# Two-layer decoder, second pass: the scores for the cross-attention maxima issued per lane instead of per pair

## What is computed

```python
logits = jnp.einsum('bhqd,bhkd->bhqk', q * SCALE, k)
logits = jnp.where(mask[:, None, None, :], -jnp.inf, logits)
attn = jax.nn.softmax(logits, axis=-1)
out = jnp.einsum('bhqk,bhkd->bhqd', attn, v)
```

## Time and profile before

| | us |
|---|---|
| median of 3 runs (3334.25 to 3343.13) | 3335.63 |
| the profiled execution | 3339.14 |
| its span, first to last instruction | 3337.6 |
| PE busy | 3049.2 (91%) |
| DVE busy | 2039.0 (61%) |
| ACT busy | 1907.7 (57%) |
| second pass, about | 915 to 2258 |

### The profile page before, as it was taken

How to read it: one execution, slowest core, us unless ns; L and a number is a source line. 1 busy time by engine, 2 the same in 40 slices (tenths; PEclk the granted TensorE clock), 3 DMA queues, 4 the chain that set the end, 5 groups by cost and what they waited for, 6 DMA issues and landing times. The chain is left out here.

```text
span 3337.6 us, 82480 instructions
## 1 busy us (share of the span) xinstructions
PE 3049.2 (91%) x31903; PEld 2442.6 (73%) x31903; DVE 2039.0 (61%) x6892; ACT 1907.7 (57%) x6449; POOL 387.0 (12%) x457
## 2 busy tenths in 40 slices
PE   6999999999888989898989898975999989999998
PEld 5777777777675757575757575754888878888886
DVE  3666667666546364646464646454677766767775
ACT  2665556665544545454545444444677767777775
POOL 1112211122000000000000000000111111111111
PEclk8999999999999999999999999986999999999999
DMA  3000000000020101010101010005001122020100
GB/s 118 17 15 17 12 13 15 17 14 20 19 66 9 33 9 33 9 33 9 33 9 33 9 33 10 9 7 202 16 15 19 17 60 61 16 63 15 18 16 10
DMA packets 63711, 95.77 MB, mean 29 GB/s; under 512 B 6962, under 2 KB 58754, under 8 KB 61778
## 3 DMA queue, kind: packets, MB, share of 16 engines
q1 hardware_dynamic: 54946, 82.74, 7.8%
q0 software_dynamic: 8368, 7.70, 1.9%
HBM read 72.04 MB, written 18.37 MB: 27 GB/s over the span
## 5 line engine op out<-in xcount | busy, mean ns | idle before, releaser
L1581 PE MATMUL bps<-BXT,Bwexp 128*128 128x112 f32 x3072 | 377.4, 279 | 6.5 <-DMA Bwexp<-in_we 4.2
L1581 PEld LDWEIGHTS bps<-BXT,Bwexp 128*128 128x128 f32 x3072 | 364.9, 195 | 16.9 <-issue 7.1
L1699 ACT ACTIVATE BPT<-bps,Blow 112x112 f32<-112x112 f32 x1024 | 350.6, 440 | 39.2 <-DVE Blow L1814 39.2
L1345 DVE CUSTOM_DVE_ANT_0 PON<-pps,PMR 112x375 f32<-112x375 f32 x512 | 251.5, 545 | 127.8 <-PE pps L1080 127.8
L1699 ACT ACTIVATION_READ_ACCUMULATOR BPT<-bps,Blow 112x1 f32 x1024 | 277.5, 294 | 0.0
L1219 ACT ACTIVATE PPT<-pps,mcol 125x896 f32<-125x896 f32 x192 | 186.3, 1006 | 155.7 <-PE pps L1101 155.7
L1659 PE MATMUL bps<-Bwexp,BPT 128*112 128x256 f32 x1024 | 239.6, 383 | 8.8 <-ACT BPT L1723 8.8
L787 POOL TENSOR_TENSOR rstd<-var,nhalf 112x1 f32<-112x1 f32 (+1 forms) x96 | 154.9, 1614 | 704.2 <-DVE var L679 413.7
L1659 PEld LDWEIGHTS bps<-Bwexp,BPT 128*112 128x112 f32 x1024 | 174.7, 177 | 51.9 <-ACT BPT L1723 14.8
L1380 POOL TENSOR_TENSOR Prstd<-Pvar,nhalf 112x1 f32<-112x1 f32 x128 | 72.0, 563 | 1190.2 <-DVE Pvar L1249 1190.2
L603 ACT ACTIVATE PT<-PT,low 112x112 f32<-112x112 f32 x512 | 190.8, 376 | 30.8 <-DVE low L762 30.2
(11 more groups left out here) (311 smaller groups left out, 6962.5 us busy)
## 6 DMA issues: line engine op xcount, KB each, us to landing
Bwexp<-in_we SPq DMA_DIRECT2D x7, 2311.0 KB, 23.7
PCX<-in_ctx SPq DMA_DIRECT2D x24, 375.0 KB
out<-BY POOLq DMA_DIRECT2D x64, 112.0 KB, 3.0
BXIN<-xmid SPq DMA_DIRECT2D x61, 112.0 KB, 2.0
Bwexp<-in_we SPq DMA_DIRECT2D x7, 770.0 KB, 5.8
Brexp<-in_re SPq DMA_DIRECT2D x7, 672.0 KB, 9.3
XIN<-in_x SPq DMA_DIRECT2D x32, 112.0 KB
CX<-in_ctx SPq DMA_DIRECT2D x32, 112.0 KB
```

Source lines behind the costliest of these rows:

```text
L1345: m = v.tensor_tensor_reduce(out=ON[s][0:T, i * LC:(i + 1) * LC], in0=bank[s][i][0:T, 0:LC], in1=MR[s][:, :], scale=1.0, scalar=-3.0e38, o ...
L1581: m = mm(o[:, j * T:(j + 1) * T], wt[:, c, n0 + j * 128:n0 + (j + 1) * 128], rhs[:, c, :], start=(c == 0), stop=(c == 1))
L1699: m = A(PT[s][0:T, h, :], bank[s][i][0:T, v * T:(v + 1) * T], ACT.Exp, scale=0.25, bias=low[s][:, h:h + 1], accum_out=sums[s][:, h:h + 1])
```

## The change

The even lane no longer issues the m pieces for both lanes. Each lane issues its own, two matmuls in two row groups, and waits for its own maxima only. What is computed is the same. The strings `act2`, `dve2`, `pe2` and `pool2` are replaced; the first and third passes stay. PE's string for the second pass has 7 constant groups in place of 40 (all of the 7 near the first two rounds); with the 3 of the third pass the program has 10.

```diff
     "pe2": (
-            "332523322330132222323232233230231230011001120102312302302030131231102312301012323023012301231520"
+            "335552233223322220133232322332030230231001121003123211232013201001123032130120132223023012301310"
...
                     for r in range(8):
                         yield None if r else b1
-                        if s % 2 == 0:
-                            for k in (s, s + 1):
-                                tallies[k].wait(mx_ready[k] if r else la_ready[k])
-                            step, (c, v) = r // 4, divmod(r % 4, 2)
-                            for k in (s, s + 1):
-                                for i in range(2):
-                                    g = rows[2 * half(k, step) + i]
-                                    m = mm(bank[k][i][0:T, 0:LC], QM[k][g, c, v, :], KT[k][g, c, :], start=True, stop=True)
-                                m.then_inc(s_psum[k], 1)
+                        t.wait(mx_ready[s] if r else la_ready[s])
+                        step, (c, v) = r // 4, divmod(r % 4, 2)
+                        for i in range(2):
+                            g = rows[2 * half(s, step) + i]
+                            m = mm(bank[s][i][0:T, 0:LC], QM[s][g, c, v, :], KT[s][g, c, :], start=True, stop=True)
+                        m.then_inc(s_psum[s], 1)
```

More of the change, by code:

```diff
@@ L67 @@
             "12030132130231230320201201010111"),
[L68 to L76, removed]
+    "act2": ("323322322201332323223323002013011230231120130100110101001210312323232323232302310231012012301301"
+            "022120123301203130321032312233230020130112302311201301001101010012103123232323232323023102310120"
+            "123013010221201233012031303210323122332300201301123023112013010011010100121031232323232323230231"
+            "023101201230130102212012330120313032103231223323002013011230231120130100110101001210312323232323"
+            "232302310231012012301301022120123301203130321032312233230020130112302311201301001101010012103123"
+            "232323232323023102310120123013010221201233012031303210323122332300201301123023112013010011010100"
+            "121031232323232323230231023101201230130102212012330120313032103231223323002013011230231120130100"
+            "110101001210312323232323232302310231012012301301022120123301203130321032312233230020130112302311"
+            "2013010011010100121031232323232323230231023101230101010101010101"),
     "act3": ("321032103210321032312301320120130332223332221103210032312313100203213302213210310310202121032100"
@@ L91 @@
             "1320123210021310030210123101021011"),
[L92 to L99, removed]
+    "dve2": ("332233220011223320032113230022132312230321320212302312330031310010101010101010112323223233223302"
+            "120100101133200321132300221323122303213202123023123300313100101010101010101123232232332233021201"
+            "001011332003211323002213231223032132021230231323003131001010101010101011232322323322330212010010"
+            "113320032113230022132312230321320212302313230031310010101010101010112323223233223302120100101133"
+            "200321132300221323122303213202123023132300313100101010101010101123232232332233021201001011332003"
+            "211323002213231223032132021230231323003131001010101010101011232322323322330212010010113320032113"
+            "230022132312230321320212302313230031310010101010101010112323223233223302120100101133200321132300"
+            "2213231223032132021230231323003131001010101010101011232323010101"),
     "dve3": ("321032103231201302103332223332120112003232321312010330310122203130132021121000323232131201033031"
@@ L115 @@
             "3320302020112130310132001202313130120202101010111"),
[L116 to L130, removed]
@@ new lines @@
+    "pe2": ("335552233223322220133232322332030230231001121003123211232013201001123032130120132223023012301310"
+            "303512301012301023102312301023101230123213012323015201320132012012322013320102103310130321032312"
+            "233203023023100112010312321123201320100112303213012013222302301230131030312301012301023102312301"
+            "023101230123213012355230120132013201201232201332010210331013032103231223320302302310011201031232"
+            "112320132010011230321301201322230320123013103031230101230102310231230102310123012321301232301201"
+            "320132012012322013320102103310130321032312233203023023100112010312321123201320100112303213012013"
+            "222303201230131030312301012301023102312301023101230123213012323012013201320120123220133201021033"
+            "101303210323122332030230231001120103123211232013201001123032130120132223032012301310303123010123"
+            "010231023123010231012301232130123230120132013201201232201332010210331013032103231223320302302310"
+            "011201031232112320132010011230321301201322230320123013103031230101230102310231230102310123012321"
+            "301232301201320132012012322013320102103310130321032312233203023023100112010312321123201320100112"
+            "303213012013222303201230131030312301012301023102312301023101230123213012323012013201320120123220"
+            "133201021033101303210323122332030230231001120103123211232013201001123032130120132223032012301310"
+            "30312301012301023102312301023101230123213012323012301010101010101010101"),
@@ L141 @@
     "pool1": ("321320103201332200113201332200113201332200113201332200113201332200113201332200113201332200113201"),
-    "pool2": ("332200112301230122233320100311012301222333201003110123012223332010031101230122233320100311012301"
-            "2223332010031101230122233320100311012301222333201003110123012301"),
+    "pool2": ("332200112302130123223320100113021301232233201001130213012322332010011302130123223320100113021301"
+            "2322332010011302130123223320100113021301232233201001130213012301"),
     "pool3": ("323321201100323322101100323322101100323322101100323322101100323322101100323322101100323322101100"
```

## The result

The changed kernel takes 3346.53 us (median of 9 runs, 3344.18 to 3348.92), the kernel before 3336.88 (9 runs), a ratio of 1.0025 with a 95% interval of 1.0016 to 1.0034: **slower by 8 to 10 us**, where +15 was forecast. The interval excludes no change at all; the size is at the edge of the 10 us that the prediction named as the least that a measurement tells. The profiled execution has a span of 3347.2 for 3337.6.

A forecast was written before the change was run, and what follows sets the result against it. PE's own work plus its waits, mostly for DVE's maxima, was taken as the bound. +2.6 us a round over eight rounds gives +21, less 6 at the end: +15, 3351 us; whole range 3303 to 3377.

The forecast's parts named there:

- The walk: Second-pass round followed piece by piece through PE's and DVE's new order, lengths from the timeline; 168.3 us for 165.7.
- stretch A: From lane 2's first step to lanes 0 and 1's first product with the values; 83.3 us with clock fall, +4.8.
- stretch B: From that first product with the values to the next round's first step; forecast 85.0 us, −2.1.
- +10.7 us a round: Added PE work when 16 pair steps (13.3 us) become 32 lane steps (24.0) in a round.
- Price of a lane step: PE time for one lane's two maxima matmuls: 0.75 us taken, 0.64 and 0.83 kept as bounds.
- the same fall and the same price, 2.7 us: PE's clock falls to half in the phase of lanes 2 and 3 as before, costing 2.7 us a round.
- They stand before waits or beside them: The 33 constant groups removed, about 0.84 us each, 28 us in all, stand at PE's waits.
- The third rival: Without constant groups a second clock fall each round at yo, ga and e2, 2.7 us; likely 3375; chance 0.10.
- The last round: Only the steps of lanes 0 and 1 are left to wait for; eight at about 2.3 us for 3.14 return 6.
- Table loads: ACT has four more a round at 1.28 us, most hidden; 1.2 us of waits found in B.

The follow-up runs named there:

- Run 8: As run 1, with maxima steps of lanes 2 and 3 issued again into the same banks where PE would idle; 3314.6 us, 0.9926 against the kernel before.
- run 1: The changed code, each lane issuing its own two matmuls, with all four strings of the kernel before; 3321.8 us, 0.9947 against the kernel before.

## Why the prediction was right in sign, and what was mis-sized

- **The walk.** Its places hold. With lane 2's first step (1497.25) at 0, m5 was put at 21.4 with 2.0 idle and came at 20.5 with 1.85; m6 at 24.1 came at 23.2; mt of lane 3 at 40.7 came at 41.3; the end of stretch A was put at 80.6 at full clock and came at 79.7; stretch B was put at 85.0 and took 85.3 (1576.99 to 1662.29). That PE work would fill the shortened waits was right: +10.7 us a round was 86 in all; the group of the steps has 93 more, and PE in all, without the groups dropped, 82.
- **Price of a lane step.** 0.75 was chosen, 0.81 measured, 1.9 us a round more for 32 steps. The Trainium skill, "TensorEngine Tiling (Array Packing)", Key Properties, states that a change of the tiling mode drains the engine, from which the prediction took 0.83. The trace is near that; that the 0.17 above the 0.64 of a matmul is a drain is not shown. The price was made up for by steps of opposite row groups side by side, and by e pieces that start under a step, which overlap more than the walk allowed: 93 us against the 101 that 0.81 for each of the 256 steps would give.
- **"I expect the same fall and the same price, 2.7 us."** The fall came, most of the price did not. From m6 to mt of lane 3, which holds nearly all of the slow stretch (clock 0.50 from 1519.5 to 1529.5), the walk at full clock has 16.6 us and the trace 18.1: 1.5 us, if the walk is right there. By the end of stretch A this is made good again, at 79.7 for 80.6. Run 8 shows 2.1 us from filling the place with the old strings. This term is the main excess of the forecast for the round shown, which takes 165.0 us, not 168.3. The idle time that the recorded text sets beside the walk is also misread: in the earlier trace rows the clock is at 0.53 from 1515 on, so of the 5.6 us that it counts ahead of the fall, the two waits behind 1515.21 (1.38 us of L1047 and 0.22) came after it.
- **"They stand before waits or beside them"**: the constant groups were costed at nothing in the forecast. This is the step that failed. They are worth 15 us in the old order, 22 to 24 in run 1 and 16 in the new. The third rival had the mechanism and the place, the waits at yo, ga and e2; it took the fall for every round at 2.7 us, 22 in all, and it comes in four of the six rounds looked at.
- **The total was partly luck.** The forecast is +2.6 us in each of eight rounds and −6 at the end. Measured are +1.7 a round in six, +6.9 in the last, −4.6 at the start and −3.2 behind the pass. Against the forecast the rounds are 11 us lower, the last round 13 higher and the two ends 8 lower, and only the sum of these errors is small, 5 us. Within the rounds, too, most of the price of the first fall is missing and that of the second, which was left out, is there.
- **The chances.** 0.48 stood on slower by over 0.3%, 0.22 on within; the ratio of 1.0025 falls just inside the second.
- **The last round**, where 6 us were to come back: they did not. The last round is 7 us longer than before (168.9 for 162.0). A stretch of half clock (0.50 from 2206 to 2215) lies in it where the kernel before has full clock; how much of the 7 us that is, and why eight lane steps gave nothing back, stays open. The 4.6 us at the start and 3.2 behind the pass were not forecast, and their cause was not looked for.
- **Table loads.** 1.2 us a round was forecast, 0.5 measured, within wide intervals. The Trainium skill ("ScalarE: Activation LUTs", What ACT_TABLE_LOAD costs) adds a drain of about 1.38 us to a load. The traces disagree: in the median a load starts 0.02 us behind the work before it, and the work behind it 1.29 us after the load, in the kernel before and in the changed one.
- **What was not asked.** The prediction priced issue and order together. Only apart do they show that the edit of the code was worth 18 us and the rest of the change lost 26, more than half of it by the groups.

## What to carry to other kernels

A change of what is issued and a change of its order should be timed apart; here the first was a gain that the second used up, with the constant groups that were dropped along with it. Matmuls in part of the array's rows cost almost the same alone as together, so issue them per consumer if that removes waits, but keep partners of different row groups next to each other in the queue. And before constant work is dropped because it does nothing, look at what the clock does in the waits it stood in.

## What was not expected of the hardware

Lane steps in two of the four row groups overlapped not only with each other but with the next pieces in the other groups. In the timeline of the changed kernel L1091 starts while L1076 still has matmuls to come:

```profile
1542.37 1.38 PE L1076 MATMUL pps<-PKT,PQM 32*112 32x375 f32 x6 [0.16 <-DVE Pmx L1341]
1543.29 0.38 PE L1091 MATMUL pps<-PMXT,msel 32*125 32x112 bf16 x6
1543.59 0.48 PE L1076 MATMUL pps<-PKT,PQM 32*112 32x375 f32 x2
```

Issuing matmuls again, ten lane steps where there had been four in the round's idle place, cost no time that the runs show, and the granted clock of the whole run was 0.975 for the 0.965 of run 1. And separating steps by one piece cost about 0.6 us a step, though PE had 12 us of idle time in 167 in run 1.
